# Opening of layer 0: chunk 0 of x normalised at once, all fused weights in six banks ahead of the steps, ScalarE's copies ahead of the descent

## What is computed

```python
xn = _layernorm(x, axis=-1)
# attention, 16 heads of 64
q = z @ wq @ fcq_w + fcq_b
k = z @ wk @ fck_w + fck_b
v = z @ wv @ fcv_w + fcv_b
scores = jnp.einsum('bihd,bjhd->bhij', q, k) / scale
attn = jax.nn.softmax(scores, axis=-1)
out = jnp.einsum('bhij,bjhd->bihd', attn, v)
return out @ fco_w + fco_b
# ffn: windowed attention (8 heads) + routed attention (8 heads), the routing by
def body(carry, _):
    a, b = carry
    sb = (s + b) / EPS
    a = EPS * (logk - jax.nn.logsumexp(sb, axis=-1, keepdims=True))
    b = -jax.nn.relu(s + a)
    return ((a, b), None)
(a, b), _ = jax.lax.scan(body, init, None, length=N_ITERS)   # 50 iterations
```

## Time and profile before

| | |
|---|---|
| runs, median (lowest to highest) | 1737.21 us (1735.13 to 1738.3) |
| the profiled execution's own time | 1740.82 us |
| its span, first to last instruction | 1739.0 us |
| busy: PE, DVE, ACT, POOL | 1565.3, 1171.2, 1003.8, 387.4 us |
| mean granted TensorE clock | 0.96 of full speed |

### The profile page before, as it was taken

How to read it: one execution, slowest core, us unless ns; L and a number is a source line. 1 busy time by engine, 2 the same in 40 slices (tenths; PEclk the granted TensorE clock), 3 DMA queues, 4 the chain that set the end, 5 groups by cost and what they waited for, 6 DMA issues and landing times. The chain is left out here.

```text
span 1739.0 us, 31909 instructions
## 1 busy us (share of the span) xinstructions
PE 1565.3 (90%) x10932; PEld 1090.2 (63%) x10932; DVE 1171.2 (67%) x3048; ACT 1003.8 (58%) x2691; POOL 387.4 (22%) x397
## 2 busy tenths in 40 slices
PE   6999999999999999899999895888979957999976
PEld 3677777666666666577877764555547723555543
DVE  4688889887777776456544434677633367999964
ACT  2588888766666666354544442143444437878945
POOL 1211000000000000100321044322443400888820
PEclk7999999999999999899999998799999978999999
DMA  8000000000000000300001022300011131333300
GB/s 264 1 1 2 1 2 2 25 1 2 1 1 2 1 2 1 114 2 1 21 18 32 2 68 83 115 1 2 20 50 56 41 87 21 86 87 90 91 19 25
DMA packets 45563, 62.49 MB, mean 36 GB/s; under 512 B 7624, under 2 KB 32016, under 8 KB 44592
## 3 DMA queue, kind: packets, MB, share of 16 engines
q1 hardware_dynamic: 40864, 51.08, 10.0%
q0 software_dynamic: 4544, 9.38, 1.5%
HBM read 49.88 MB, written 15.75 MB: 38 GB/s over the span
## 5 line engine op out<-in xcount | busy, mean ns | idle before, releaser
L584 ACT ACTIVATE probs<-psum_all,pair_negmax 128x256 f32<-128x256 f32 x512 | 235.9, 473 | 170.5 <-DVE pair_negmax L747 94.2
L2181 POOL TENSOR_TENSOR weighted<-state,c_all 128x512 f32<-128x512 f32 x128 | 163.6, 1298 | 78.6 <-DVE state L2191 64.8
L747 DVE TENSOR_REDUCE pair_negmax<-psum_all 128x2 f32<-128x512 f32 x192 | 123.7, 686 | 67.6 <-PE psum_all L474 67.6
L2191 DVE TENSOR_TENSOR_SCAN state<-decay,psum_all 128x512 f32<-128x512 f32 x128 | 149.0, 1200 | 14.3 <-PE psum_all L2109 11.5
L773 DVE TENSOR_SCALAR probs<-probs,pair_recip 128x256 f32<-128x256 f32 x512 | 146.6, 351 | 4.5
L474 PE MATMUL psum_all<-keys,queryT 64*128 64x256 f32 x1024 | 143.8, 400 | 1.4 <-DVE values L729 0.9
L595 ACT ACTIVATE probsT<-psum_all 128x512 f32<-128x512 f32 x256 | 140.2, 612 | 0.8 <-PE psum_all L485 0.7
L501 PE MATMUL psum_all<-probsT,values 128*64 128x256 f32 x1024 | 138.8, 392 | 0.0
L485 PE MATMUL psum_all<-ident,probs 128*128 128x128 f32 x1024 | 133.8, 274 | 1.8 <-ACT probsT L595 1.8
L485 PEld LDWEIGHTS psum_all<-ident,probs 128*128 128x128 f32 x1024 | 120.3, 141 | 16.3 <-issue 3.6
L474 PEld LDWEIGHTS psum_all<-keys,queryT 64*128 64x128 f32 x1024 | 92.3, 189 | 51.4 <-issue 42.5
(11 more groups left out here) (364 smaller groups left out, 3265.1 us busy)
## 6 DMA issues: line engine op xcount, KB each, us to landing
c_all<-c_rows SPq DMA_DIRECT2D x64, 256.0 KB, 3.3
slots<-slot_fill_dram SPq DMA_DIRECT2D x2, 2535.0 KB, 14.1
ring<-slots SPq DMA_DIRECT2D x18, 260.0 KB, 2.9
keys<-found SPq DMA_DIRECT2D x16, 256.0 KB, 4.4
up<-up_dram SPq DMA_DIRECT2D x1, 2048.0 KB, 7.9
down<-down_dram SPq DMA_DIRECT2D x1, 2048.0 KB, 12.3
up<-up_dram SPq DMA_DIRECT2D x1, 1408.0 KB, 6.0
found<-values,dest POOLq DMA_INDIRECT x78, 2.2
```

The lines of the kernel that those rows point to most:

```text
L584: nc.scalar.activation(k.probs[:, 2 * (u % PAIR_BUF) + j, t, :], k.psum[score_bank(u, j)][:, SEQ * t:SEQ * (t + 1)], ACT.Exp, bias=k.pair_ ...
L747: nc.vector.reduce_max(k.pair_negmax[:, u % 2, SUB * j:SUB * (j + 1)], src, AXX, negate=True).then_inc(s.negmax_ready, 1)
L2181: nc.gpsimd.tensor_tensor(w.weighted[:, u % RING, :], w.state[:, u % RING, :], w.c_all[:, u // L3_DC % C_RING, :], ALU.mult)\
L2191: nc.vector.tensor_tensor_scan(w.state[:, u % RING, :], w.decay[:, u % L3_RING, :, :].rearrange("p b n -> p (b n)"), k.psum[u % PARTS_RING ...
```

## The change

Four things are changed in `layer0_stage` and in the tables of jobs.

1. VectorE normalises chunk 0 right after its statistics; the statistics of chunks 1 to 3 and the second scales follow, and chunks 1 to 3 are normalised in steps 0, 1 and 2, ahead of these steps' late jobs. ScalarE's roots of chunks 1 to 3, the root of the scales and the table load come after the copies of `before`.
2. All four fused weights and fold_turn are in `before`, which has nine jobs now, in banks 7, 6, 5, 4, 3, 2, 7, 6, 5; each job from the seventh on waits for the copy of the one six ahead. The late jobs of the first steps move up: fold 0; fold 1 and x_turn 1; bias and x_turn 2; x_turn 3; logits (steps 0 to 4; before in steps 2 to 6, with fused and fold_turn ahead).
3. In a step, ScalarE does its copies of jobs ahead of the descent's exponential and logarithm, no longer behind them.
4. The descent starts at step 6 (it was 7), and what hangs on it (scores, weights, ranks, choice) moves with it by one step.

```diff
--- before.py
+++ after.py
@@ -203,7 +203,7 @@
 PBUF = 4
 SEQS = BATCH
 GROUPS = 2 * SEQS
-DESCENT_FROM = 7
+DESCENT_FROM = 6
 DESCENT_LAST = DESCENT_FROM + DESCENTS - 1
 ROUTE = Names(scores=DESCENT_LAST, weights=DESCENT_LAST + 1, turn=DESCENT_LAST + 2, columns=DESCENT_LAST + 2,
               ranks={DESCENT_LAST + 5 + n: (2 * n, 2 * n + 1) for n in range(BATCH)}, choice=DESCENT_LAST + 5 + BATCH)
@@ -214,9 +214,9 @@
 
     U = GROUPS * PAIRS
     before, early, late = [], [[] for _ in range(U + 4)], [[] for _ in range(U + 4)]
-    before += [("x_turn", 0, 0), ("fused", 0, 0), ("fused", 0, 2), ("pair", 0, 0), ("pair", 0, 1), ("values", 0, 0)]
-    for step, jobs in enumerate(([("fused", 0, 1), ("x_turn", 0, 1)], [("fused", 0, 3), ("fold_turn", 0, 0)], [("fold", 0, 0), ("fold", 0, 1)],
-                                 [("bias", 0, 0)], [("x_turn", 0, 2)], [("x_turn", 0, 3)], [("logits", 0, 0)])):
+    before += [("x_turn", 0, 0), ("fused", 0, 0), ("fused", 0, 2), ("fused", 0, 1), ("fused", 0, 3), ("fold_turn", 0, 0), ("pair", 0, 0), ("pair", 0, 1),
+               ("values", 0, 0)]
+    for step, jobs in enumerate(([("fold", 0, 0)], [("fold", 0, 1), ("x_turn", 0, 1)], [("bias", 0, 0), ("x_turn", 0, 2)], [("x_turn", 0, 3)], [("logits", 0, 0)])):
         late[step] += jobs
     for g in range(GROUPS):
         ffn = g >= SEQS
@@ -253,7 +253,7 @@
 
     def job_bank(job):
 
-        return k.psum[JB - number[job] if number[job] < len(before) else JB]
+        return k.psum[(7, 6, 5, 4, 3, 2, 7, 6, 5)[number[job]] if number[job] < len(before) else JB]
 
     def is_ffn(g):
         return g >= SEQS
@@ -386,6 +386,8 @@
                     n, jb = number[job], job_bank(job)
                     if n >= len(before):
                         wait_saved(pe, order[n - 1])
+                    elif n >= 6:
+                        wait_saved(pe, before[n - 6])
                     if what == "x_turn":
                         pe.wait_ge(s.x_normed, CT * (i + 1))
                         for j in range(CT):
@@ -607,15 +609,13 @@
                     nc.scalar.activation(k.route_log[:, :], k.route_sum[:, :], ACT.Ln).then_inc(s.route_act, 1)
 
                 root(0)
-                root(1)
-                do(before[0])
-                root(2)
-                root(3)
+                for job in before:
+                    do(job)
+                for c in range(1, CHUNKS):
+                    root(c)
                 act.wait_ge(s.moments_ready, 2)
                 nc.scalar.activation(w.norm_scale[:, :, :], w.norm_scale[:, :, :], ACT.Sqrt).then_inc(s.scales_ready, 1)
                 nc.scalar.preload_act_table_set("natural_log_exp_and_others")
-                for job in before[1:]:
-                    do(job)
                 for u in steps:
                     if u < U:
                         exponentials(u)
@@ -623,13 +623,13 @@
                         save_turned(u - T_AFTER)
                     if 0 <= u - V_AFTER < U:
                         save_out(u - V_AFTER)
+                    for job in early[u] + late[u]:
+                        do(job)
                     if DESCENT_FROM <= u < DESCENT_LAST:
                         descend(u - DESCENT_FROM)
                     if u == ROUTE.scores:
                         act.wait_ge(s.scored, 1)
                         nc.scalar.activation(k.route_exp[:, :], k.logits[:, :], ACT.Exp).then_inc(s.exped, 1)
-                    for job in early[u] + late[u]:
-                        do(job)
 
             @block.vector
             def _(dve):
@@ -799,10 +799,9 @@
                         descend_dve_first(nc, k).then_inc(s.route_dve, 1)
 
                 chunk_statistics(0)
+                chunk_norm(0)
                 for c in range(1, CHUNKS):
                     chunk_statistics(c)
-                    chunk_norm(c - 1)
-                chunk_norm(CHUNKS - 1)
                 second_scales()
                 for job in before:
                     do(job)
@@ -815,9 +814,11 @@
                         add_output((u - O_AFTER) // PAIRS)
                     if 1 <= u <= U:
                         normalise(u - 1)
+                    if u in (0, 1, 2):
+                        chunk_norm(u + 1)
                     for job in late[u]:
                         do(job)
-                    if u == 2:
+                    if u == 3:
                         dve.wait_ge(s.null_weighted, 1)
                         nc.vector.reduce_sum(w.null_w[:, :], w.null_product.rearrange("p (h e) -> p h e", e=HD), AXX).then_inc(s.null_weighted, 1)
                     if u == DESCENT_FROM - 1:
```

## The result

| | before | changed |
|---|---|---|
| median (lowest to highest), 4 runs each on one chip | 1737.76 us (1735.13 to 1739.94) | 1718.41 us (1717.9 to 1720.37) |
| the profiled execution's own time, its span | 1740.82, 1739.0 us | 1718.38, 1716.5 us |
| mean granted TensorE clock | 0.960 | 0.968 |

The ratio is 0.9891, with a 95% interval of 0.9874 to 0.9909: the changed kernel takes 1.1% less, 19 us. The forecast was 1718.5.

What follows compares the result with a forecast made beforehand. TensorE, 90% busy, bounds the whole kernel, but not layer 0's opening. Edits 1 and 2 give 11.9 us after 2 for the clock, edit 3 6.8, edit 4 0: 18.7 off, 1718.5 us, range 1714.5 to 1725.5.

Steps and rivals of the forecast that it cites:

- Ahead of the first scores: Opening of layer 0: first scores start at 19.25 us instead of 27.47, a gain of 8.2 us.
- My 16: Opening: TensorE is through by 16 us with turning x, four fused weights and fold_turn.
- The short 1.3: Opening: the removed wait is replaced by TensorE waiting for VectorE, about 1.3 us long.
- Rival (b): Clock already down at 12 to 16 us: scores at 24.5, gain 12.5 us, 1724.7 us; chance 0.10.
- Step 1: Layer 0, maxima to maxima: VectorE 5.1, then x_turn 0.65 and scores 1.2, together 7.0 us.
- the 2 us for the clock: Steps 0 to 2: x_turn, one scores and one pair at the low clock cost 2 us.
- VectorE 3.32 + 1.09 + 0.69 = 5.1: Step 1 on VectorE: maxima, pair copies and normalising 3.32, a chunk of xn 1.09, a fold copy 0.69 us.
- Rival (a): Clock stays up through steps 0 to 2: the 2 us are kept, gain 20.7, 1716.5 us; chance 0.17.
- my argument against it there: Before 36 us in the old trace, the clock fell without an idle stretch, against the skill's rule.
- rival (c): Copies ahead of the descent free nothing, as ScalarE is too full: gain 11.9, 1725.3 us; chance 0.08.
- the ends of -1 and +1: Descent a step earlier: ranks of 1.9 us move between steps; effect between -1 and +1 us, taken as 0.
- Rival (d): Slower: gaps of steps 0 to 2 hold the clock at 1.2 GHz into steps 3 to 7; 1742.5 us; chance 0.03.

Runs made afterwards that it cites:

- copies_first: The kernel before with only ScalarE's job copies moved ahead of the descent; 1728.38 us, against 1738.56 for the kernel before.
- norm0_only: The kernel before with only chunk 0 normalised at once and x_turn 0 copied ahead of the roots of chunks 1 to 3; 1736.04 us.
- fill_both: fill with GpSimd's five instructions moved behind the bias addition and chunk 2 normalised behind step 1's fold copy; 1727.04 us, ratio 0.9862 to the kernel before.
- fill: The changed kernel with three unread 512-column matmuls in TensorE's gap ahead of the first scores; 1733.15 us, kernel before 1754.02 on that chip.
- after2: The changed kernel run once more with no edit; 1719.59 us, against 1738.56 for the kernel before in that set.

## Why the prediction was right, and where it wasn't

**The sum.** 18.7 us were forecast. The trace of layer 0 shows 19.04, and the medians 1737.8 and 1718.4 differ by 19.4. The profiled execution, which I put at 1722.1, took 1718.4; 3.5 us of that error I put down to the scatter of later layers, since the profile of before was the one with the longest tail (1061.1 us). The sum was also helped by what the profile of before happened to lose to the clock in steps 0 to 2: against copies_first, which lost nothing there, the same change would have shown 7.99 + 6.86 + 0.56 = 15.4 us in layer 0.

**Ahead of the first scores** the forecast was 19.25, measured 18.93. The reason held too: TensorE is through with its jobs at 16.0, the fused weights take 0.93 us each, the table load is hidden, and the wait left is for VectorE's values. It is 2.9 us long, where I had written 1.3. My 16 was added up from the turn, four weights and fold_turn alone, and with two pair jobs of 1 us behind it 1.3 are left. On the trace these three end at 13.70: the warm-up ended at 9.14, not 10.11, the weights took 3.70 where I allowed up to 4.48, and fold_turn 0.65 and not 1.1. The short 1.3 made me count the gap as harmless for the clock. That the changed kernel's profile passed it unharmed was luck: in four of seven profiles of nearly this order step 0 cost 2.4 to 2.7 us more. Rival (b), a low clock from 12 to 16 us, is out: the granted clock is 1.00 there in this trace, and norm0_only makes its two weights at full clock too, from 9.76 to 11.74 (its clock falls at 14.2, when TensorE has stood still for over 2 us).

**Steps 0 to 8.** Step 0: 4.40 as forecast. Step 2: 7.48 (7.4). Step 3: 6.29 (6.5). Step 4: 8.01 (8.1). Steps 5 to 7: 13.38 (13.4). Step 8: 5.05. Step 1 is the one that failed: 7.0 and a share of the 2 us for the clock were forecast, 9.86 measured. It splits into

- 1.68 us of VectorE normalising beside GpSimd (2.82 - 1.14), a term that I didn't have at all. The step of the prediction that failed is "VectorE 3.32 + 1.09 + 0.69 = 5.1": the 3.32 came from step 3 of the kernel before, where GpSimd does nothing. Bringing the step forward moved VectorE into 26.7 to 29.5 us, where GpSimd works as soon as its weights are there: L364 starts between 26.9 and 27.4 us in every profile that has it in this place;
- 1.41 us of clock, from x_turn to the maxima;
- 6.77 us for the rest, where I had 7.0.

So the first two edits gained 11.67 us instead of 11.9: the missing 1.7 us was offset by a clock term of 1.4 instead of 2, by a start 0.3 earlier and by steps some tenths shorter. The sum came out closer than its terms.

**The clock.** That it would fall in steps 0 to 2 was right in the changed kernel, and its price of about 2 us was a fair guess for 1.41. Where it falls isn't settled by the order alone: at the gap ahead of the first scores it stayed up in three profiles and fell in four of nearly the same kernels, and the order of the kernel before showed opening times 3.7 us apart. Rival (a) was no outcome of this change, but fill_both shows that it can be had: with no gap over about 1.1 us the clock stayed up, in its one profile. The Trainium skill (TensorE: Matmul & The Clock Gate, Part 1) gives a stretch in which the engine was idle as what takes the clock back down. The changed kernel's fall, 3.1 us into 3.40 us of standing, agrees with it, and my argument against it there was built on gaps that were too short. The fall in the kernel before, where no gap exceeded about 1.1 us, isn't explained by it, and copies_first passed the same gaps with none.

**Edit 3** gave 6.86 us (forecast 6.8), by the mechanism forecast: the copies in the descent's place, the descent where ScalarE would have waited for maxima. copies_first rules rival (c) out. **Edit 4** gave 0.56 us, within the ends of -1 and +1 and not the 0 that I took. **Rival (d)**, a clock that stays low on into steps 3 to 7, didn't happen: it is back at 34.3 us in the changed kernel, and at 36.4 us at the latest in every other profile that has the new order.

**What stays open**: why the clock falls at the gap ahead of the first scores in one execution and not in another. The runs show only that it does, and that a filled gap (four profiles) never had it. At the gap ahead of x_turn 1 the moment differs as well: the clock fell 0.9 us into the gap in fill, 3.1 us into it in the changed kernel, and 0.6 us after its end in after2. No run fills that gap while the first one is filled too, so that the gap of step 1 causes its fall is argued from fill_both alone.

## What to carry to other kernels

When a change makes one engine's work earlier, look at what the *other* engines do in the new stretch, and at what ties them to a time of their own: here GpSimd was tied to the landing of weights, and the step moved into it. A duration taken from another place of the trace holds only if the neighbours are the same there. Two small causes of one gap can be worth far more together than singly (4.3 us here, against 1.0 and 0.6); take them away together before judging either. And where the clock falls in one profile and not in another of the same order, look at more than one profile before a difference of a few us is put down to an edit.
